# A graph attention layer on one core: GpSimd instead of VectorE turns four batches of variances into inverse deviations

## What is computed

```
h  = relu((x - mean(x)) / sqrt(var(x) + 1e-5))      # per node, x is 8192 x 128
Wh = h @ W                                          # W is 128 x 128
f1 = Wh @ a[:128];  f2 = Wh @ a[128:]
e  = leaky_relu(f1[:, None] + f2[None, :], 0.2)     # 8192 x 8192
e  = where(adj == 0, -inf, e)                       # adj: 8192 x 8192 int32
out = x + softmax(e, axis=1) @ Wh
```

## Time and profile before

| what | us |
|---|---|
| median of three executions | 784.26 |
| lowest and highest of them | 783.3 and 784.69 |
| the profiled execution | 783.76 |
| span in its profile, first to last instruction | 781.3 |
| busy in the span: TensorE | 760.6 (97%) |
| VectorE | 737.0 (94%) |
| ScalarE | 578.6 (74%) |
| GpSimd | 442.3 (57%) |

### The profile page before, as it was taken

The page is one execution under the profiler, slowest core; times in us unless marked ns, Lnnn a source line. Parts: engine busy times, 40 slices in busy tenths (PEclk is TensorE's granted clock), DMA queues, the critical chain, the costliest instruction groups (busy, mean ns, idle before and its releaser), DMA issues.

```text
span 781.3 us, 23331 instructions
## 1 busy us (share of the span) xinstructions
PE 760.6 (97%) x8731; PEld 692.2 (89%) x8731; DVE 737.0 (94%) x1197; ACT 578.6 (74%) x1138; POOL 442.3 (57%) x501
## 2 busy tenths in 40 slices
PE   6899899999999999999999999999999999999996
PEld 5789799999999999999999999999999999999986
DVE  7998899999999999999999999999999999999997
ACT  5889877777777777777777777777777777777762
POOL 8787855645645565564556556465655646564510
PEclk9999999999999999999999999999999999999999
DMA  9999999999999999999999999999999999997100
GB/s 174 174 105 109 89 108 118 108 117 106 98 96 103 106 87 107 91 97 97 98 111 88 106 91 96 96 101 109 88 106 90 96 97 99 110 89 79 18 16 17
DMA packets 46149, 75.98 MB, mean 97 GB/s; under 512 B 2594, under 2 KB 11428, under 8 KB 46116
## 3 DMA queue, kind: packets, MB, share of 16 engines
q0 software_dynamic: 41088, 67.12, 89.9%
q1 hardware_dynamic: 4880, 8.39, 3.2%
q10 hardware_dynamic: 148, 0.07, 0.0%
HBM read 272.70 MB, written 4.19 MB: 354 GB/s over the span
## 4 chain that ended last, share of the span: by engine, by line
PE 89%; DVE 5%; ACT 2%; POOL 1%; issue 1%; DMA 1%; DVEq 0%; ACTq 0%; POOLq 0%
PE acc L454 55%; PE acc L458 28%; DVE wt_ring L961 4%; PE stage L445 3%; PE stage L419 1%; DMA masks<-in_adj_dram 1%; PE stage L428 1%; POOL xn L262 1%; PE stage L401 1%; POOL tmp L309 0%; ACT marks L706 0%; DVE pairs L951 0%; ACT marks L664 0%; PE stage L436 0%; ACT wh L628 0%
## 5 line engine op out<-in xcount | busy, mean ns | idle before, releaser
L961 DVE SCALAR_TENSOR_TENSOR wt_ring<-stage,packed,marks 128x512 f32<-128x512 f32 x1024 | 697.5, 743 | 31.6 <-PE acc L458 12.1
L454 PE MATMUL acc<-pairs,wt_ring 128*128 128x258 f16 x4096 | 719.4, 274 | 5.4 <-DVE pairs L951 3.5
L458 PE MATMUL acc<-pairs,wt_ring 128*128 128x129 f16 x4096 | 697.6, 220 | 0.0
L454 PEld LDWEIGHTS acc<-pairs,wt_ring 128*128 128x128 f16 x4096 | 399.0, 98 | 61.7 <-DVE pairs L951 5.1
L458 PEld LDWEIGHTS acc<-pairs,wt_ring 128*128 128x128 f16 x4096 | 400.1, 98 | 4.5
L706 ACT ACTIVATE marks<-codes 128x512 uint16<-128x512 uint8 x480 | 274.7, 620 | 13.0
L696 ACT ACTIVATE codes<-stage 128x512 uint16<-128x512 uint8 x240 | 142.8, 595 | 156.4 <-PE stage L445 156.0
L270 POOL DMA_DIRECT2D masks<-in_adj_dram x120 | 87.5, 729 | 229.7 <-PE stage L445 208.4
L289 POOL TENSOR_TENSOR masks<-masks 128x512 int32<-128x512 int32 x120 | 150.6, 1280 | 1.3
L298 POOL TENSOR_TENSOR masks<-masks 128x256 int32<-128x256 int32 x120 | 87.5, 734 | 56.0 <-ACT masks L689 55.1
L689 ACT ACTIVATE masks<-masks 128x512 uint16<-128x512 uint16 x120 | 74.8, 624 | 0.8 <-POOL masks L289 0.4
(11 more groups left out here) (75 smaller groups left out, 215.4 us busy)
## 6 DMA issues: line engine op xcount, KB each, us to landing
masks<-in_adj_dram POOLq DMA_DIRECT2D x120, 512.0 KB, 8.9
masks<-in_adj_dram POOLq DMA_DIRECT2D x16, 256.0 KB, 22.3
out_dram<-xm SPq DMA_DIRECT2D x15, 256.0 KB, 7.8
xm<-in_x_dram SPq DMA_DIRECT2D x1, 1536.0 KB, 13.2
xm<-in_x_dram SPq DMA_DIRECT2D x2, 512.0 KB, 5.9
xm<-in_x_dram SPq DMA_DIRECT2D x1, 1024.0 KB, 10.0
xm<-in_x_dram SPq DMA_DIRECT2D x2, 256.0 KB, 3.1
out_dram<-xm SPq DMA_DIRECT2D x4, 64.0 KB, 2.6
```

The lines of the kernel that those rows point to most:

```text
L454: return nc.tensor.matmul(acc[:, r, 0:2 * E1], wtv[:, w, r, 1, :], pairv[:, t, :, 0:E1], start=st, stop=end)
L458: return nc.tensor.matmul(acc[:, r, E1:2 * E1], wtv[:, w, r, 0, :], pairv[:, t, 0, 0:E1], start=False, stop=False)
L961: nc.vector.scalar_tensor_tensor(out=wtq[:, t % NW], in0=e_row, scalar=packed[:, t, 1:2], in1=edges[:, k], op0=ALU.max, op1=ALU.min).then_ ...
```

## The change

GpSimd gets its own `inverses(k)` and calls it in steps 0, 1, 4 and 8, behind `mix(b + 2)` and ahead of `normalise(b + 4)`. VectorE no longer calls its own for batches 2 to 5; it keeps batches 0 and 1, ahead of the steps. [...] ScalarE's `root` and everything else stay.

```
+            def pool_then(ins):
+                pool_steps[0] += 1
+                ins.then_inc(s["pool_step"], 1)
+                pool.wait_ge(s["pool_step"], pool_steps[0])
+
+            def inverses(k):
+                sl = slice(BATCHES[k][0] * PACK, BATCHES[k][1] * PACK)
+                both, root, square, rstd, shift = (small[:, n, sl] for n in (1, 3, 4, 5, 6))
+                pool.wait_ge(s["root_ready"], k + 1)
+                nc.gpsimd.tensor_scalar(both, stats[:, sl, 2], 1.0 / D, EPS, ALU.mult, ALU.add)
+                pool_then(nc.gpsimd.tensor_tensor(square, root, root, ALU.mult))
+                pool_then(nc.gpsimd.tensor_tensor(square, square, both, ALU.mult))
+                pool_then(nc.gpsimd.tensor_scalar(square, square, 0.5, -1.5, ALU.mult, ALU.add))
+                pool_then(nc.gpsimd.tensor_tensor(square, square, root, ALU.mult))
+                nc.gpsimd.tensor_scalar(rstd, square, -1.0, None, ALU.mult)
+                nc.gpsimd.tensor_tensor(shift, stats[:, sl, 1], square, ALU.mult).then_inc(s["ln_ready"], 1)
...
                 if b == UN - 1:
                     join(NC, 1)
+                if b in ROOTS:
+                    inverses(ROOTS[b])
                 if b + 4 < NQ:
                     normalise(b + 4)
...
                 if b == 0:
                     low_part(b)
-                elif b - 1 in ROOTS and b > 1:
-                    inverses(ROOTS[b - 1])
                 weights(1, b, range(HALF, PACK))
...
                 if b == 0:
-                    inverses(ROOTS[b])
                     next_group(1)
```

More of the change, by code:

```diff
@@ L156, in gat_kernel @@
             "transposed", "weighted", "used", "acc_done", "acc_free",
-            "g_fin", "g_step", "g_shift", "g_probs", "g_tp", "g_t", "g_sums")}
+            "pool_step", "g_fin", "g_step", "g_shift", "g_probs", "g_tp", "g_t", "g_sums")}
         adj_loaded = [s[f"adj_loaded{c}"] for c in range(NC)]
@@ L264, in normalise @@
                 ins.then_inc(s["xn_pool"], 1)
+            pool_steps = [0]
+            def pool_then(ins):
[13 more added lines that the diff above has]
+                nc.gpsimd.tensor_tensor(shift, stats[:, sl, 1], square, ALU.mult).then_inc(s["ln_ready"], 1)
             def load_half(q, c, h):
```

## The result

The changed kernel takes 786.6 us (median of 8 executions, 785.55 to 787.38) against 784.43 for the kernel before: a ratio of 1.0027, with an interval of 1.0016 to 1.0037, or 1.3 to 2.9 us slower. The forecast was 783.8, in a range of 782.4 to 786.2. The profiled execution has a span of 784.5 us against 781.3.

The account below looks back on a forecast made before the run. In the first 90 us TensorE's gaps were taken to end with VectorE's low half, GpSimd's new chain limiting the gain. 0.88 us earlier less 0.44 of hold-up, about 0.45: 784.26 - 0.45 = 783.8 us, range 782.4 to 786.2.

Parts of the forecast that it names:

- What bounds the kernel: First 90 us: TensorE's gaps ahead of steps 2, 5 and 9, together 3.06 us, end with VectorE's low half.
- the first rival: GpSimd's chain is short, 1.06 us, and VectorE's gain arrives: batch 5 1.85 us earlier, 782.4 us; chance 0.18.
- The path from `normalise` to TensorE: From `normalise` through `scaled` and ScalarE's `keep` to TensorE's `features(g, 1)`: 3.32 us together.
- What the new chain costs: GpSimd, `mix` to `normalise`: seven instructions and four waits, 1.60 us in batches 4 and 5, 1.45 in 2 and 3.
- A term on the other side: VectorE's low half slows GpSimd in steps 5 and 9 by 0.44 us each, counted once of two times.
- The sums by batch: Batch 2's chain ends 0.19 us earlier; `features(4, 1)` 1.02, `features(7, 1)` 0.75 and `features(11, 1)` 0.88 us earlier.
- The last load of x: Step 4: VectorE waits for this load until 34.3, so step 4 gains 0.47 us at most.
- The long chain: Between `mix` and `normalise` in all four batches: at 2.3 us, 1.6 us late, 785.9 us; chance 0.20.
- a hold-up in each: Rival: VectorE and GpSimd hold each other up in every batch, 0.44 us per chain, 784.8 us; chance 0.20.
- a chain over 2.3 us: Sign of a wrong forecast: GpSimd's chain takes over 2.3 us; under 1.25 us was named as well.
- The estimate of 2.3 us: GpSimd's chain at twice the 1.15 us of VectorE's batch 4, making the kernel slower by 1.6 us.

Follow-up runs that it names:

- the short chain: The changed kernel with two GpSimd instructions in place of seven, Newton step and sign of the shift left out: 782.01 us, 0.9975 of the kernel before.

## Why the prediction was wrong

**What bounds the kernel** was right: TensorE's three gaps end with VectorE's low half, and a short chain turns them into a gain: 1.9 and 2.2 us with two instructions on GpSimd, 1.4 with one on VectorE, about the size of the first rival, 1.9. The path from `normalise` to TensorE, 3.32 us, came out to 0.01 in batches 3, 4 and 5 (29.96 to 33.29, 45.80 to 49.12, 64.61 to 67.93).

**What the new chain costs** is the first term that failed. The tensor-tensors (0.22 us forecast, 0.19 to 0.22 measured) and the waits (0.09 and 0.09: a step begins 0.29 us after one of 0.20) were right. The tensor-scalars were not: 0.20 to 0.26 us for 0.12. The fixed part of 0.07 came from a straight line through two different instructions, one with two scalars per partition and one without. That makes 1.79 us for 1.54 in batch 3, and about 2.0 for 1.69 in batches 4 and 5 (2.53 less the hold-up).

**A term on the other side** is the second, and the larger. I counted 0.44 us once of two times; it came in all four batches: 0.46 to 0.51 us in three chains, and 0.45 in the `mix` ahead of the fourth; the `mix` at 33.09 in between lost 0.47 more. GpSimd's timeline in the kernel before had more of them than the two places I looked at:

```profile
37.05 1.86 POOL L262 TENSOR_SCALAR xn<-xm,small 128x128 f32<-128x128 f32 x3
...
61.66 1.48 POOL L309 TENSOR_TENSOR tmp<-wh,tmp 128x512 f32<-128x512 f32 x1
```

They took 1.30 and 1.04 us elsewhere; a low half ran beside each (38.08 to 38.76 and 61.51 to 62.23). With VectorE free of `inverses`, the low half comes earlier, and right into GpSimd's new work. The two runs with the low half's input in PSUM show it: without hold-ups the change costs 0.58 us of stretch in place of 2.71.

**The sums by batch** hold with the measured terms in them. Batch 2's chain is 0.85 us longer than forecast, batch 3's chain and `mix` 0.25 + 0.45: from 1.02 earlier to 0.53 later; `features(4, 1)` was 0.58 later, counted from `mix(2)`. For batch 4, `mix` ended 1.21 later in place of 0.7 earlier, since GpSimd waited for no other engine from 20.74 to 54.40 and so carried every delay on, the one at 33.09 with them; and the chain was 0.84 longer: -0.75 + 1.91 + 0.84 = 2.00 later, as measured (49.12 - 20.74 against 46.48 - 20.10). For batch 5 the start was 2.00 later in place of 0.75 earlier, 2.75: -0.88 + 2.75 + 0.84 = 2.71 later, as measured. The path was right but not alone: the direct wait for xn, which I had left out, came first in batches 2 to 5. In the run with the swap on ScalarE, without the second wait, `features(11, 1)` comes 0.46 us earlier (a stretch of 46.73), but the same half of the next step only 0.09, and the time doesn't tell it from nothing.

**The last load of x** was forecast at 34.3 and is seen at 34.2 in the short chain, and at 34.9 in the version with one instruction on VectorE. In the changed kernel it played no part, as everything was later than that.

**The rivals.** The long chain was to be slower by 1.6 us from 2.3 us on, and three of the four chains took 2.39 to 2.53; a hold-up in each was the reason that they did, and a chain over 2.3 us was one of the signs of being wrong that I had named. I had given each a chance of its own, 0.20, as if they excluded one another, and put the range's end at the long chain's start. Together they make the 2.7 us that the profile has; the range had no room for it. The estimate of 2.3 us from the rule of the Trainium skill (GPSIMD Engine Reference, section 4.1, Engine selection), two-input instructions about twice as slow on GpSimd, came near these three chains by luck: at 8 or 16 elements a tensor-tensor takes 0.19 to 0.22 us on GpSimd and 0.17 on VectorE (the row of line 906 above). The sharing of interfaces that the Trainium skill names (GPSIMD Engine Reference, section 1, Specifications) is what the runs bear out, with 0.66 to 0.72 us for 0.20 beside a low half with two inputs in SBUF and 0.22 beside one with an input in PSUM.

**Not settled:** whether the longer steps alone, without hold-ups, make the change slower. The 0.58 us of stretch come from one profile each, and the times don't resolve them. Nor does a run show why the straight line priced the tensor-scalars too low.

## What to carry to other kernels

Work moved to a less busy engine is paid where that engine's own result is awaited: count from the instruction in front of it to the last engine in the queue behind it, and not by shares of busy time. Two rivals that lengthen the same chain add up; a range has to hold their sum. When a two-input instruction of VectorE moves earlier, look at what GpSimd runs there, and count a hold-up wherever they now meet.

## What the runs showed of the hardware

- VectorE's low half, with its two inputs in SBUF, and a GpSimd instruction hardly run together: GpSimd's small ones take 0.66 to 0.72 us in place of 0.20 when a low half of 0.69 runs, and a low half behind a row of GpSimd instructions took up to 2.29 us. With one of its inputs in PSUM neither happens.
- A VectorE instruction with one tensor in SBUF can wait for GpSimd too: line 905 took 0.52 us beside `mix`, to 41.46, where `mix` ended at 41.42, and 0.16 in the kernel before with the low half's input in PSUM, where it began at 41.46, behind a `mix` that ended at 41.41.
- A GpSimd tensor-tensor or tensor-scalar on 8 to 16 elements takes 0.19 to 0.26 us, and the next one that waits for it starts some 0.09 later.
- After a gap of 2.44 us TensorE's clock went to 0.50 for some 3 us; gaps of 1.42 and 0.61 in the kernel after, and of 1.90 in the version with one instruction on VectorE, left it at 1.00; a gap of 1.90 in that version with the earlier load of x was followed by 0.50 from 42 to 45 us. What decides isn't shown.
- The first part of the adjacency matrix came at other times in each profile: ScalarE's first scaling of edges began at 9.31 us before, at 9.80 after, and between 8.57 and 11.23 in the other runs. A difference of 0.5 us between two single profiles can be that alone.
